# A two-layer gated cross-attention and expert kernel: packed attention values, own scores in column tiles, early unread products, and reordered steps

## What is computed

```python
x = x + tanh(g_xattn[0]) * L0_xattn(layernorm(x), ctx, ctx)    # 16 heads of 8, softmax attention over 64 keys
x = x + tanh(g_ffn[0])   * L0_ffn(layernorm(x))                # 8 experts, the best 2, silu(xW1)*(xW2) @ W3
x = x + tanh(g_xattn[1]) * L1_xattn(layernorm(x), ctx)         # see below
x = x + tanh(g_ffn[1])   * L1_ffn(layernorm(x))                # 8 experts, the best 2, gelu, rank 64
# L1_xattn(e, q):
Sim  = (e @ w1)[:, :, None] + (q @ w2)[:, None, :] + einsum('bid,bjd->bij', e * w3, q) + b
hq   = softmax(Sim, axis=2) @ q
hc   = softmax(max(Sim, axis=2), axis=1) @ e                   # one row for each sequence
out  = concat([e, hq, e * hq, e * hc]) @ W_qv + b_qv
```

## Time and profile before

| | |
|---|---|
| median of 3 runs | 516.65 us (515.8 to 518.7) |
| profiled execution | 515.37 us, span 513.6 us |
| TensorE busy | 473.2 us (92%) |
| VectorE busy | 395.6 us (77%) |
| ScalarE busy | 307.9 us (60%) |
| GpSimd busy | 220.1 us (43%) |

### The profile page before, as it was taken

How to read it: one execution, slowest core, us unless ns; L and a number is a source line. 1 busy time by engine, 2 the same in 40 slices (tenths; PEclk the granted TensorE clock), 3 DMA queues, 4 the chain that set the end, 5 groups by cost and what they waited for, 6 DMA issues and landing times. The chain is left out here.

```text
span 513.6 us, 13958 instructions
## 1 busy us (share of the span) xinstructions
PE 473.2 (92%) x4366; PEld 384.4 (75%) x4366; DVE 395.6 (77%) x1566; ACT 307.9 (60%) x750; POOL 220.1 (43%) x300
## 2 busy tenths in 40 slices
PE   2688999999999999999899999988998989899997
PEld 1356777777777777778678888757897877787896
DVE  5778888888889889677675667676798886777974
ACT  1567788777777777555456655474544547453553
POOL 3322055555554334456200177472677762214320
PEclk9999999999999999899989999998999999999999
DMA  8701011111111110134465664220000221000011
GB/s 243 301 11 53 13 32 43 37 36 31 36 36 33 33 54 22 38 89 120 122 172 166 175 177 121 80 78 19 26 22 17 58 61 43 12 0 1 2 42 41
DMA packets 45023, 34.60 MB, mean 67 GB/s; under 512 B 5922, under 2 KB 41122, under 8 KB 44708
## 3 DMA queue, kind: packets, MB, share of 16 engines
q1 hardware_dynamic: 30036, 20.55, 13.4%
q0 software_dynamic: 4128, 8.40, 5.8%
q10 hardware_dynamic: 10800, 4.92, 3.4%
HBM read 21.85 MB, written 11.99 MB: 66 GB/s over the span
## 5 line engine op out<-in xcount | busy, mean ns | idle before, releaser
L493 POOL DMA_INDIRECT sent<-xr,rowu x60 | 59.7, 995 | 46.7 <-DVE rowu L1047 28.3
L509 POOL DMA_INDIRECT yg<-done,gidx x64 | 64.0, 999 | 33.8 <-issue 17.3
L1746 PE MATMUL bank<-QK 128*64 128x256 f32 x512 | 70.6, 397 | 7.9 <-ACT QK L625 5.4
L468 POOL TENSOR_TENSOR ve<-mv,half 128x4 f32<-128x4 f32 (+1 forms) x40 | 8.8, 219 | 118.9 <-DVE mv L845 117.8
L637 ACT ACTIVATE PT<-bank 128x512 f32<-128x512 f32 x64 | 36.4, 602 | 32.4 <-PE bank L1712 31.7
L1305 DVE TENSOR_TENSOR act<-sil,bank 128x256 f32<-128x256 f32 x71 | 29.8, 420 | 29.6 <-ACT sil L687 28.0
L1746 PEld LDWEIGHTS bank<-QK 128*64 128x64 f32 x512 | 32.3, 139 | 26.2 <-ACT QK L625 6.8
L924 DVE TENSOR_REDUCE mx<-bank 128x8 f32<-128x512 f32 x64 | 44.0, 687 | 9.2 <-PE bank L1746 9.2
L687 ACT ACTIVATE sil<-bank 128x256 f32<-128x256 f32 x71 | 27.3, 384 | 35.4 <-PE bank L1903 35.3
L1919 PE MATMUL bank<-f0w_s,aT 128*128 x284 | 45.1, 282 | 0.8 <-DVE yb L1311 0.8
L928 DVE TENSOR_TENSOR Pr<-bank,mx 128x512 f32<-128x512 f32 x64 | 43.7, 683 | 1.6
(11 more groups left out here) (264 smaller groups left out, 1256.2 us busy)
## 6 DMA issues: line engine op xcount, KB each, us to landing
xb<-sent SPq DMA_DIRECT2D x71, 64.0 KB
done<-yb ACTq DMA_DIRECT2D x71, 64.0 KB
cT<-ctx_t_dram SPq DMA_DIRECT2D x16, 128.0 KB, 2.2
f0w_s<-f_w_dram SPq DMA_DIRECT2D x1, 2048.0 KB, 11.4
Pr<-ctx_t_dram SPq DMA_DIRECT2D x8, 256.0 KB
QK<-ctx_tok_dram SPq DMA_DIRECT2D x8, 256.0 KB
out_dram<-xs SPq DMA_DIRECT2D x8, 256.0 KB, 2.3
xs<-x_dram SPq DMA_DIRECT2D x2, 512.0 KB, 6.4
```

The lines of the kernel that those rows point to most:

```text
L493: nc.gpsimd.indirect_dma_start(sent, bass.IndirectOffsetOnAxis(ap=rowu[:, s, 2 * k + c:2 * k + c + 1], axis=0), rows[:, c, :], None).then_ ...
L509: nc.gpsimd.indirect_dma_start(yg[:, s, j, :], None, done[0:NBH * P, :] if u < UG else done, bass.IndirectOffsetOnAxis(ap=gidx[:, s, j:j + ...
L1746: last = mm(bank[g % 2][L * b:L * (b + 1), 256 * p:256 * (p + 1)], QT[:, s, g, t:t + L], Kb[:, s, :, t:t + L], start=True, stop=True)
```

## The change

- **Values.** `wv_eo` holds only the 8 heads of one parity, 64 columns. `a_v` streams 64 columns and writes 256 in place of 512. `Vb` is zeroed once by GpSimd (in place of `wv_eo`), and `a_vs` is two copies of 64 partitions x 256.
- **Unread products.** Once the fills are done (now 10), TensorE issues 28 products of 256 columns on zeros, with 32, 64 and 128 rows and 64 weight columns, ahead of the bias matmul.
- **SyncE.** The tails are zeroed two in each of the steps 16 to 19.
- **GpSimd.** Three gathers of the fourth unit stand ahead of the roots of unit 1.
- **VectorE.** `r_pos` and `r_own` of unit 14 move from step 5 to 4; `c_rmx(0)`, `c_nmx(0)` of step 65 go ahead of that step's statistics; `both(3, 0)` moves behind `c_ehc(0, 0)`.
- **Own scores.** `c_own` has weights of 32 equal columns, each of the four matmuls on its own 32 partitions; `mcol`, `bm`, `brow`, `bs`, `br`, `wrow` have 128 partitions, and `c_mt` and `c_wt` are 128 wide.

```diff
-        wv_eo = sb("wv_eo", [P, 2, D])
+        wv_eo = sb("wv_eo", [P, 2, D // 2])
...
-                if TAIL <= t < TAIL + E:
-                    zero_after(t - TAIL)
+                if TAIL <= t < TAIL + E // 2:
+                    zero_after(2 * (t - TAIL))
+                    zero_after(2 * (t - TAIL) + 1)
...
-            nc.gpsimd.memset(wv_eo[:], 0.0).then_inc(fill, 1)
+            nc.gpsimd.memset(Vb[:], 0.0).then_inc(fill, 1)
...
-            nc.gpsimd.memset(w1c[:], 0.0).then_inc(fill, 1)
...
             fetch(2, range(8))
+            fetch(3, range(3))
             rstd(2, 1, 4)
-            fetch(3, range(8))
+            fetch(3, range(3, 8))
...
-                nc.vector.tensor_copy(Vb[:, s, :, :, 0:16],
-                                      bank[5][:].rearrange("p (b h d) -> p b h d", b=4, d=16)).then_inc(S("a_vs"), 1)
+                for e in range(2):
+                    keys = slice(L * e, L * (e + 1))
+                    last = nc.vector.tensor_copy(Vb[keys, s, :, :, DH * e:DH * (e + 1)],
+                                                 bank[5][keys, 0:2 * P].rearrange("p (b h d) -> p b h d", b=4, d=DH))
+                last.then_inc(S("a_vs"), 1)
...
-                nc.vector.tensor_scalar(mcol[:], rmx[:], gate[:, 4:5], None, ALU.add).then_inc(S("c_mcol"), 1)
+                nc.vector.tensor_scalar(mcol[:], rmx[:].unsqueeze(2).to_broadcast([P, 4, 32]), gate[:, 4:5], None, ALU.add).then_inc(S("c_mcol"), 1)
...
                 if t == 4:
                     r_ln(n, n % 2)
-                if t == 5:
                     r_pos(n - 1)
                     r_own(n - 1)
+                if t == 5:
                     kept(n - 1)
...
             c_rsm(0, 0)
-            both(3, 0)
             c_bs(0)
...
             c_ehc(0, 0)
+            both(3, 0)
...
+            def unread_rows(n):
+                for _ in range(2):
+                    for r in range(P // n):
+                        for c in range(2):
+                            some = slice(n * r, n * (r + 1))
+                            mm(bank[r][L * c:L * (c + 1), 0:2 * P], QK[some, 0, L * c:L * (c + 1)], QK[some, 1, 0:2 * P], start=True, stop=True)
+
+            pe.wait_ge(fill, 10)
+            for n in (32, 64, 128):
+                unread_rows(n)
+
+            pe.wait_ge(prep, 7)
+            mm(bank[7][:, 0:D], bvb[:], wo_s[:], start=True, stop=True).then_inc(prep_pe, 1)
...
-                        last = mm(bank[5][L * e:L * (e + 1), P * b:P * (b + 1)], cT[:, s, L * b:L * (b + 1)],
+                        last = mm(bank[5][L * e:L * (e + 1), L * b:L * (b + 1)], cT[:, s, L * b:L * (b + 1)],
                                   wv_eo[:, e, :], start=True, stop=True)
...
-                    mm(bank[OWN_BANK[u // UG]][0:4, P:2 * P], w1c[:, c, :], xc(u)[:, P * c:P * (c + 1)], start=c == 0, stop=False)
+                    mm(bank[OWN_BANK[u // UG]][32 * c:32 * (c + 1), P:2 * P], w1r[:], xc(u)[:, P * c:P * (c + 1)], start=True, stop=False)
...
-                mm(bank[OWN_BANK[u // UG]][0:4, P:2 * P], mcol[:], ident, start=False, stop=True).then_inc(S("c_mt"), 1)
+                mm(bank[OWN_BANK[u // UG]][:, P:2 * P], mcol[:].rearrange("p c r -> p (c r)"), ident, start=False, stop=True).then_inc(S("c_mt"), 1)
...
-                nc.tensor.transpose(bank[OWN_BANK[u // UG]][:, 4:8], wrow[:], cst[0:4, C_ID:C_ID + 4]).then_inc(S("c_wt"), 1)
+                nc.tensor.transpose(bank[OWN_BANK[u // UG]][:, 2 * P:3 * P], wrow[:], ident).then_inc(S("c_wt"), 1)
```

More of the change, by code:

```diff
@@ L231, in flamingo @@
         rsm = sb("rsm", [P, 4])
-        mcol = sb("mcol", [P, 4])
-        bm = sb("bm", [4, 2])
-        brow = sb("brow", [4, 2, L])
-        bs = sb("bs", [4, 2])
-        br = sb("br", [4, 2])
-        wrow = sb("wrow", [4, P])
+        mcol = sb("mcol", [P, 4, 32])
+        bm = sb("bm", [P, 2])
+        brow = sb("brow", [P, 2, L])
+        bs = sb("bs", [P, 2])
+        br = sb("br", [P, 2])
+        wrow = sb("wrow", [P, P])
         wbd = sb("wbd", [P, 4, 2])
@@ L243, in flamingo @@
         ehq = sb("ehq", [P, 4 * P])
-        w1c = sb("w1c", [P, 4, 4])
+        w1r = sb("w1r", [P, 32])
         ehc = sb("ehc", [P, 2, 4 * P])
@@ L418, in _ @@
                 if u == 1:
-                    sp.wait_ge(fill, 11)
+                    sp.wait_ge(fill, 10)
                     for e in range(E):
@@ L459, in _ @@
             nc.gpsimd.memset(QK[:, 0:U4 // 2, :], 0.0).then_inc(fill, 1)
-            nc.gpsimd.memset(w1c[:], 0.0).then_inc(fill, 1)
             pool.dma_start(f0g_s[:], f0_wg).then_inc(ld_f0g, 16)
-            pool.wait_ge(fill, 11)
+            pool.wait_ge(fill, 10)
             def rstd(k, u, n):
@@ L643, in _ @@
             a.wait_ge(prep, 3)
-            a.wait_ge(fill, 11)
+            a.wait_ge(fill, 10)
             def r_xts(v):
@@ L879, in _ @@
             nc.vector.tensor_scalar(rsum[:, 1, :], rowv[:, R_BQV:R_BQV + D], tg[:, 1:2], None, ALU.mult).then_inc(prep, 1)
+            v.wait_ge(fill, 6)
             for s in range(2):
@@ L887, in _ @@
             v.wait_ge(ld_attn, 64)
-            v.wait_ge(fill, 11)
+            v.wait_ge(fill, 10)
             nc.vector.tensor_copy(bvb[:], colv[:, BV:BV + 1].to_broadcast([P, P]))
@@ L892, in _ @@
             for e in range(2):
-                last = nc.vector.tensor_copy(wv_eo[:, e, :].rearrange("p (h e d) -> p h e d", e=2, d=DH)[:, :, e, :],
+                last = nc.vector.tensor_copy(wv_eo[:, e, :].rearrange("p (h d) -> p h d", d=DH),
                                              wv_s[:].rearrange("p (h e d) -> p h e d", e=2, d=DH)[:, :, e, :])
             last.then_inc(prep, 1)
-            nc.vector.tensor_copy(w1c[:].rearrange("p c m -> p (c m)")[:, 0:16:5], colv[:, W1S:W1S + 1].to_broadcast([P, 4])).then_inc(prep, 1)
+            nc.vector.tensor_copy(w1r[:], colv[:, W1S:W1S + 1].to_broadcast([P, 32])).then_inc(prep, 1)
             def split_biases():
@@ L1360, in c_bsub @@
                 v.wait_ge(S("c_bm"), u + 1)
-                nc.vector.tensor_tensor(brow[:], maxima(u), bm[:].unsqueeze(2).to_broadcast([4, 2, L]), ALU.subtract).then_inc(S("c_bsub"), 1)
+                nc.vector.tensor_tensor(brow[:], maxima(u), bm[:].unsqueeze(2).to_broadcast([P, 2, L]), ALU.subtract).then_inc(S("c_bsub"), 1)
             def c_bs(u):
@@ L1487, in _ @@
                     nc.vector.tensor_scalar(wqv_g[:], wqv_s[:], tg[:, 1:2], None, ALU.mult).then_inc(prep, 1)
+                if t == NB - 6:
+                    c_rmx(0)
+                    c_nmx(0)
                 for u in range(3):
@@ L1503, in _ @@
                     norm(0, 4, xn[:, 0], "c_ln", 2)
-                if t == NB - 6:
-                    c_rmx(0)
-                    c_nmx(0)
                 if t == NB - 4:
@@ L1704, in _ @@
             mm = nc.tensor.matmul
-            pe.wait_ge(prep, 7)
-            mm(bank[7][:, 0:D], bvb[:], wo_s[:], start=True, stop=True).then_inc(prep_pe, 1)
             def transposes(done, dst, src, n):
```

8 lines of the change are left out of this document (4 added, 4 removed).

## The result

Over 20 runs each on one chip the changed kernel took 513.68 us against 517.14 us before, ratio 0.9938 with a 95% interval of 0.9919 to 0.9958. On a second chip it was 512.79 against 517.23, ratio 0.9893 (0.9864 to 0.9921). So it is 0.6 to 1.1% faster, by these two ratios 3.2 to 5.5 us of 517 (by the ends of their intervals, 2.2 to 7.0). The profiled execution took 511.92 us, of which the span is 510.1, against 515.37 and 513.6 before: -3.5 where the prediction had -7.8. The direction was right, the size under half.

The account below looks back on a forecast made before the run. It took TensorE to bound the attention loop, VectorE the opening, and engine round trips or SyncE's queue the expert blocks. Terms -5.0 + 0.6 - 1.1 + 1.0 - 0.5 - 1.2 - 1.6 = -7.8 gave 508.8 us from 516.65; range 505.0 to 513.0.

Parts of the forecast that it names:

- Part 1, packed values: Attention loop: halved value-projection columns save 0.40 us a unit in 13 units, first three lose 0.1 each; -5.0 us.
- Rival (a): Attention loop: VectorE takes over because the half copies cost more, leaving 0.1 to 0.15 us a unit; 512.3 us, chance 0.15.
- Part 2, early products: Opening: unread products ahead of the bias matmul end near 9.85 us and delay it and VectorE's chain; +0.6 us.
- (b): Opening: row parts of the array don't overlap for the unread products; +3.9 us, 512.7 us, chance 0.10.
- (f): Opening: the 28 unread products run singly, ending near 19.0 us, so the kernel gets slower; 517.9 us, chance 0.04.
- Part 3, rank: Expert blocks, step 5: ranks taken one step earlier remove TensorE's 1.09 us wait for VectorE's running count; -1.1 us.
- Part 4, zeroing: Expert-block load queue: two zeroings a step lengthen the stall to 3.1 us in place of 1.66; +1.0 us.
- Part 5, own scores: Own scores on four column tiles: -0.5 us at unit 0, -1.2 together at units 2, 3 and 7.
- Rival (d): Own scores: each column switch drains the array, so 2.7 us of gain go; 511.5 us, chance 0.08.
- Part 6, entry: Entry to the cross stage: moved adds let the values' product start 0.65 us earlier, own scores get shorter; -1.6 us.

Follow-up runs that it names:

- values_back: Changed kernel with the value projection as before it (128 columns with zeroed halves, one VectorE copy): 515.88 us, ratio 0.9975 to the kernel before.
- act_values: Changed kernel with both copies of the packed values on ScalarE in place of VectorE: 507.14 us, ratio 0.9792 to the kernel before.
- short_unread: Changed kernel with only the 32-row and 64-row unread products (48 of 56 records): 511.44 us, ratio 0.9869 to the kernel before.
- rank_back: Changed kernel with the last but one unit's ranks back at step 5: one execution, profiled 517.75 us.
- zero_one: Changed kernel with one region's tail zeroed a step in eight steps, as before it: 510.30 us, ratio 0.9859 to the kernel before.
- best_pairs: Same as best_short but with the tails zeroed two a step: 505.75 us, ratio 0.9780 to the kernel before.
- own_back: Changed kernel with the cross stage's own scores as before it, four products on four rows one after another: 515.08 us, ratio 0.9923 to the kernel before.
- both_back: Changed kernel with the fourth unit's two adds back ahead of the first cross unit's row sums: one execution, 510.54 us.
- before_early: Kernel before with the 56 early unread products alone added: 517.52 us against 517.33, ratio 1.0010.
- none_again: Changed kernel without its unread products, run again beside the changed kernel on one chip: 508.91 us, ratio 0.9829 to the kernel before.
- between: Changed kernel with the last eight unread products (128-row set) behind the bias product instead of ahead: 512.08 us, ratio 0.9877 to the kernel before.
- no_unread: Changed kernel without its 56 unread products, first run: 510.23 us, ratio 0.9856 to the kernel before.
- best_short: Changed kernel with 48 early products, value copies on ScalarE, one zeroing a step, fourth unit's adds in front: 503.05 us, ratio 0.9716 to the kernel before.
- before: The kernel before the change, in the trace that the prediction used: profiled 515.37 us; 517.14 us in the first comparison.
- after: The changed kernel, first comparison: 513.68 us, ratio 0.9938 to the kernel before, profiled 511.92 us.
- before_again: The kernel before, unchanged, profiled and timed once more: ratio 1.0001, profiled 517.05 us.
- after_again: The changed kernel, unchanged, run again on the second chip: 512.79 us, ratio 0.9893 to the kernel before.
- best_none: Same as best_short but without any unread product: 505.15 us, ratio 0.9756 to the kernel before.

## Why the prediction came out wrong, step by step

**Part 1, packed values: -5.0 predicted, about -2.2 measured.** The term for TensorE was right to 0.01 us (0.42). The term for VectorE failed: "two overlap a little, so some 0.77 together: 0.09 more". The copies take 0.85 and their successor starts 0.88 behind their start; in the kernel before it started 0.61 behind the one copy (124.36 to 124.97): 0.27 more, three times the estimate. That used up what the prediction had left of the slack at the third scores product, 0.1 ("the earlier TensorE takes 0.42 of it and the copy 0.09"). Rival (a) named this place; what it left of the gain, 0.1 to 0.15 a unit, was too little, since 0.28 remained. The other mistake is in the units: the prediction charged three units 0.1 each and let 13 gain 0.40. The intervals say +0.30, +0.29, +0.06 for the first three and +0.27 at the table's unit, where VectorE also ends last, only -0.06 behind it and -0.4 in the last two. Of the 2.8 us by which this part fell short the eight steady units make 0.9, the table's unit and the one behind it 1.0, and the first three 0.45; the last two intervals gave their 0.40 each, and the thirteenth unit lies behind the last a_v. values_back and act_values both show that the copies are the cause.

**Part 2, early products: +0.6 predicted, +2.4 in the traces.** Number, overlap and end of the products were right; rivals (b) and (f) fell. The step that failed is that it stopped at VectorE, which "slips with it" by 0.6 (its own ends, 10.3 for 9.58, give 0.7). VectorE slipped by 0.81, since the bias product at 9.90 was read at 10.42 in place of 9.61. And it left out what TensorE does meanwhile: it had finished sooner, stood for 2.13 us, and went on at the 1.2 GHz level, for 1.6 us more. The prediction knew the price of that level and used it only for the products themselves. That the late product is the cause is shown by short_unread; that the idle time behind it brings the clock down is read from the traces (1.63 us and the clock stayed, 2.12 and 2.13 and it fell), not shown by a run that changes only that. The Trainium skill's page "TensorE: Matmul & The Clock Gate", section "Part 1: The HAM clock gate", calls the slow start run-variable; the traces agree, with one late opening of 27.78 where TensorE had waited only 0.40.

**Part 3, rank: -1.1 predicted**, 1.12 by rank_back, 1.3 to 1.4 between the traces. Right. That half of it is returned at the load queue, as by rank_back, was not foreseen.

**Part 4, zeroing: +1.0 predicted**, bounds -0.7 and +2.5. The step time was right (3.54 for 3.6). The stall came a block ahead of the load that the prediction works out, at 19: the load issued at 244.96 let TensorE go on at 248.15, 3.2 later, where the prediction took the zeroing's landing of 1.8. At 1.90 the stall was shorter than the 3.1 of the forecast. The size depends on what it is compared with: +0.3 and -0.4 between the two pairs of traces, in which the kernel before has its own stall with a low clock, 1.65 by zero_one with 0.9 given back at block 53, 3.4 by best_pairs with 1.2 given back and 2.7 in the medians. The mechanism held. The low clock behind the stall, which the prediction had counted on the side of before, stands in the changed kernel too (0.57 from 248 to 250 us).

**Part 5, own scores: right**, 0.6 to 0.7 at unit 0. Units 2, 3 and 7 were predicted at 1.2; own_back has 0.69 for units 2 and 3 and 0.5 for unit 7. Rival (d) fell.

**Part 6, entry: the sum of -1.6 came, and more** (-2.2 and -3.5 from block 64 to cross unit 1 in the table), but not for the reason given. The scores' 1.87 to 0.42 carries it (1.53 by own_back), and in the second pair the kernel before lost 1.3 more there to its low clock. "Moved behind c_ehc, this lets the product start 0.65 earlier" was right in its number by luck: the product starts 1.38 us sooner in the trace, 0.67 of it relative to the blocks, but in both_back, with the adds in front, it starts just as soon. The wait for the gather is gone there too, which leaves the earlier fetch as its likely cause (it was not undone by itself), the adds were covered by ScalarE's exponentials, and moving them cost 0.3 to 0.4.

What stays open: the size of the change itself, between 3.2 and 5.5 us on two chips; how much of an opening's 2 us reaches the median, for before_early lost none and none_again gained 3.9; and the earlier maximum at step 65 and the three gathers moved ahead, which no run undid by themselves.

## What to carry to other kernels

An operation split into halves over the partitions isn't cheaper in time: each half costs what its elements per partition cost, so a saving on the bounding engine must be checked unit by unit against the engine that pays, and not only in the steady period. Work put ahead of an idle stretch to raise the clock must end before the first operand that something else waits for; here the last eight products cost 2.5 us by the first value projection, and whether the 48 before them bring anything stayed open. Then look for the next queue that can cover a gain: in the kernel before, blocks that came 2.2 us late were 0.4 us late behind the load queue's stall. And before a step is moved out of a wait, look whether a wait for another engine stands there anyway: then the move frees nothing and delays what it lands in front of.

## What the runs showed of the hardware

- Two copies of 64 partitions and 256 elements took 419 ns each on VectorE and 380 ns each on ScalarE, against 425 ns for VectorE's operation on 128 partitions and 256 elements.
- 48 records of unread products on 32- and 64-row parts of the array, of 256 columns, took 3.93 us. The last eight, on all rows, took 1.98 at the slow level (between).
- Four products on four column tiles took 0.42 to 0.43 us, against 1.04 for four on the same columns, both at the full level.
- The granted clock was found at its lower level in four places: in the opening; behind most load stalls of 1.66 to 2.31 us, but not behind one of 2.02 (no_unread) and not behind those of 1.11 (best_short, before_early); at the first expert blocks (0.72 over 212 to 218 us in before and after, 1.00 in before_again and act_values); and at the entry to the cross stage (before_again lost 1.3 us more there than before; in after and after_again the clock is 1.00). In the first 26 us the column can read 1.00 while the products last 1.98 in place of 1.08 (before, between, best_none), so there the durations tell it and the column doesn't.
